# Gated cross attention and a routed feed-forward layer: two halves of a small product set apart among accumulating matmuls

## What is computed

```python
x = x + tanh(g_xattn) * xattn(layernorm(x), ctx, ctx, mask, wq, wk, wv, wo)
x = x + tanh(g_ffn)   * ffn(layernorm(x), weight, bias, gate_w, in_channel_scale, out_channel_scale)

def xattn(...):                       # 32 heads in 16 pairs
    attn = softmax(rope(q) @ rope(k).T / sqrt(128) + mask)
    return (attn @ v) in heads' order @ wo        # wo: (4096, 1024)
```

## Time and profile before

| | before |
|---|---|
| median of three executions | 1468.59 us |
| profiled execution, its own time | 1468.77 us |
| its span, first to last instruction | 1467.0 us |
| TensorE busy | 1446.3 us, 99% |
| VectorE, ScalarE, GpSimd busy | 68%, 39%, 49% |
| mean granted clock of TensorE | 0.997 |
| TensorE's share of the chain that ended last | 89% |

### The profile page before, as it was taken

One profiled execution on the slowest core, in us unless ns is written; L12 is line 12 of the kernel. 1 busy time (PEld: TensorE's weight loads), 2 busy tenths in 40 slices (PEclk: granted clock), 3 DMA queues, 4 the chain that ended last, 5 costly groups with the idle time before them and its releaser, 6 DMA issues.

```text
span 1467.0 us, 21329 instructions
## 1 busy us (share of the span) xinstructions
PE 1446.3 (99%) x6800; PEld 1197.1 (82%) x6800; DVE 998.9 (68%) x2141; ACT 570.1 (39%) x927; POOL 719.9 (49%) x594
## 2 busy tenths in 40 slices
PE   7999999999999999999999989999999999999998
PEld 6988888888888888888888867888888888877786
DVE  6858888888888888888888876636246247436653
ACT  6922222222222222222222258438348348225551
POOL 6935554554555545545555456426226226036554
PEclk9999999999999999999999999999999999999999
DMA  8822122212221222122212298888998989943321
GB/s 309 289 101 65 39 80 74 69 52 70 79 70 43 79 71 71 50 71 79 71 43 72 72 312 274 292 263 275 353 353 268 369 272 298 302 152 111 113 79 65
DMA packets 114898, 226.40 MB, mean 154 GB/s; under 512 B 12272, under 2 KB 23024, under 8 KB 114704
## 3 DMA queue, kind: packets, MB, share of 16 engines
q1 hardware_dynamic: 110224, 210.03, 44.7%
q10 hardware_dynamic: 4608, 15.53, 2.9%
HBM read 167.84 MB, written 57.67 MB: 154 GB/s over the span
## 4 chain that ended last, share of the span: by engine, by line
PE 89%; issue 3%; DVE 2%; POOL 2%; DMA 2%; SPq 1%; ACT 1%; POOLq 0%; ACTq 0%
PE bank L52 19%; PE bank L53 19%; PE bank L54 19%; PE bank L966 8%; PE bank L967 8%; PE bank L968 8%; PE bank L990 5%; POOL last_rows L1424 1%; PE bank L1005 1%; SPq L727 1%; DMA w_raw<-in_wo 1%; DVE stats L293 1%; DMA w_raw<-in_wkv 1%; DVE x_lo L324 1%; PE xt_ps L152 0%
## 5 line engine op out<-in xcount | busy, mean ns | idle before, releaser
L52 PE MATMUL bank<-x_hi,w_hi 128*128 128x512 f32 x1024 | 398.5, 389 | 0.3 <-issue 0.3
L54 PE MATMUL bank<-x_hi,w_lo 128*128 128x512 f32 x1024 | 398.3, 389 | 0.0
L53 PE MATMUL bank<-x_lo,w_hi 128*128 128x512 f32 x1024 | 398.3, 389 | 0.0
L1363 POOL TENSOR_TENSOR q_lo<-rot,q_hi 128x512 fp32r<-128x512 f32 x128 | 165.4, 1293 | 184.0 <-ACT q_hi L1126 183.1
L52 PEld LDWEIGHTS bank<-x_hi,w_hi 128*128 128x128 f32 x1024 | 192.2, 188 | 40.4 <-issue 0.5
L53 PEld LDWEIGHTS bank<-x_lo,w_hi 128*128 128x128 f32 x1024 | 192.2, 188 | 39.9
L54 PEld LDWEIGHTS bank<-x_hi,w_lo 128*128 128x128 f32 x1024 | 192.2, 188 | 39.8
L1126 ACT CAST q_hi<-rot 128x512 fp32r<-128x512 f32 x128 | 79.5, 621 | 346.2 <-DVE rot L1487 254.2
L1429 POOL TENSOR_TENSOR w_lo<-w_raw,w_hi 128x512 fp32r<-128x512 f32 x100 | 127.1, 1292 | 169.5 <-ACT w_hi L1178 169.5
L1559 DVE TENSOR_TENSOR project<-bank,project 64x512 fp32r<-64x512 f32 x128 | 87.5, 684 | 144.8 <-ACT project L1186 142.8
L1370 POOL TENSOR_TENSOR pt_lo<-pt,pt_hi 128x512 fp32r<-128x512 f32 x64 | 82.5, 1290 | 153.7 <-ACT pt_hi L1136 153.6
(11 more groups left out here) (143 smaller groups left out, 2656.4 us busy)
## 6 DMA issues: line engine op xcount, KB each, us to landing
project<-probs_scratch SPq DMA_DIRECT2D x160, 256.0 KB, 6.8
w_raw<-in_wo SPq DMA_DIRECT2D x100, 256.0 KB, 4.6
p_left<-probs_scratch SPq DMA_DIRECT2D x96, 256.0 KB, 5.7
w_raw<-in_wq SPq DMA_DIRECT2D x32, 512.0 KB, 5.2
probs_scratch<-pt_hi SPq DMA_DIRECT2D x64, 256.0 KB, 2.6
probs_scratch<-pt_lo SPq DMA_DIRECT2D x64, 256.0 KB, 3.2
last_rows<-in_x SPq DMA_DIRECT2D x8, 1024.0 KB, 8.4
x_scratch<-last_rows SPq DMA_DIRECT2D x8, 1024.0 KB, 9.1
```

The source lines that it names most:

```text
L52: pe.matmul(out, hi, rhs_hi, start=first, stop=False, **kw)
L53: pe.matmul(out, hi, rhs_lo, start=False, stop=False, **kw)
L54: return pe.matmul(out, lo, rhs_hi, start=False, stop=last, **kw)
L1363: nc.gpsimd.tensor_tensor(q_lo[:, c], rot[:, c], q_hi[:, c].bitcast(F32), ALU.subtract).then_inc(q_lo_ready, 1)
```

## The change

A helper `halves` issues, for h 0 and 1: half h of the upcoming product, if there is one, and then two of the four tiles of rows of the sum. All three kinds of phases call it. Product and sum are the same instructions as before; a sum is now two calls of `probs_times` with two tiles each, and each call issues its three waits.

In phase 0 the product also stands at another place in relation to the sum: before, product hp + 2 came behind sum hp; now its halves come in front of and in the middle of sum hp. At hp 0 the sum has already been issued, so only the product is. The other engines' and queues' orders are as before.

```diff
--- before.py
+++ after.py
@@ -971,6 +971,14 @@
                 if t == NACC - 1:
                     last.then_inc(av_done, 1)
 
+            def halves(phase, hp, upcoming, rows=True):
+
+                for h in range(2):
+                    if upcoming is not None:
+                        values_wo(upcoming, h)
+                    if rows:
+                        probs_times(phase, hp, (2 * h, 2 * h + 1))
+
             def products(i, j, steps):
 
                 for step in steps:
@@ -1066,21 +1074,16 @@
             values_wo(1, 1)
             probs_times(0, 0, (1, 2, 3))
             for hp in range(HP):
-                if hp >= 1:
-                    probs_times(0, hp)
-                if hp + 2 < HP:
-                    for h in range(2):
-                        values_wo(hp + 2, h)
+                halves(0, hp, hp + 2 if hp + 2 < HP else None, hp >= 1)
             for phase in range(1, PHASES):
                 rnd, long = phase // PB, phase % PB == 0
                 for hp in range(HP):
+                    upcoming = None
                     if long and hp + 3 < HP:
-                        for h in range(2):
-                            values_wo(rnd * HP + hp + 3, h)
+                        upcoming = rnd * HP + hp + 3
                     if not long and hp in SHORT_VW and rnd + 1 < ROUNDS:
-                        for h in range(2):
-                            values_wo((rnd + 1) * HP + SHORT_VW[hp], h)
-                    probs_times(phase, hp)
+                        upcoming = (rnd + 1) * HP + SHORT_VW[hp]
+                    halves(phase, hp, upcoming)
                     if phase == LAST:
                         first_block(hp)
```

## The result

Twenty executions of each kernel gave a median of 1472.55 us after the change (1470.20 to 1477.42) and 1469.24 us before it (1467.74 to 1473.37). The ratio is 1.002, with a 95% interval of 1.0014 to 1.0025: the change costs 2.1 to 3.7 us, 2.9 in the middle; the two medians are 3.3 us apart. The profiled execution of the changed kernel took 1471.23 us, 2.46 us more than that of before (1468.77), and its span is 1469.4 us.

The account below looks back on a forecast made before the run. TensorE was taken as the bound. Gaps of 1.68 + 0.81 + 1.15 = 3.64 us replacing 1.62 gave +2.0, taken as +2.2: 1471.0 from the profile, 1470.8 from the median, stated 1470.9; range 1468.7 to 1473.3 us.

Parts of the forecast that it names:

- the forecast's own case: Whole kernel: the main case, 1470.8 to 1471.1 us, chance 0.50.
- the replay: Phase 0 from 872.58 us, recomputed with the rows' durations: 3.64 us of gaps in place of 1.62, +2.0 us.
- (3,0): Phase 0, product 3, half 0: waits for the drain of (2,0) until 874.18, gap 1.60 + 0.08 us.
- (4,0): Phase 0, product 4, half 0: waits for the drain of (3,0) until 879.07, gap 0.73 + 0.08 us.
- (11,0): Phase 0, product 11, half 0: waits for the drain of (10,0) until 908.78, gap 1.07 + 0.08 us.
- a later landing, a delay passed through the loads: Phase 0: drain (4,1), about 0.3 us later, can pass through the weights' loads to pair 11; upper value +2.3.
- (11,1) no longer waits: Phase 0, product 11, half 1: comes 2.04 us later, so its gap of 0.76 us goes.
- phases 1 to 7 cost nothing: Phases 1 to 7: parted halves cost and give nothing, as products there have slack.
- Extra waits at 0: All sums: 381 more waits on TensorE, taken as 0, upper bound 1.3 us.
- The clock rival: Phase 0, after 873 us: the granted clock falls to 0.5; 1472 to 1473.7, about 1472.4 us, chance 0.25.
- the half one: Phase 0, within the clock rival's 0.25: a fall half as long as 6.8 us, +1.0 us besides the 2.2.
- the DMA's matter: Phase 0, weights of pair 11: issued at 898.00, in ScalarE's hands at 905.32, not expected to get earlier.

Follow-up runs that it names:

- The second lot: The changed kernel run again, unmodified, six executions against the kernel before: 1474.31 us, ratio 1.0031.
- whole, no gaps: Kernel before with rows' load later, pair 2's weights earlier, ScalarE draining product 15 before casting weights of pairs 16 and 17: 1466.92 us, ratio 0.9988.
- parted, no gaps: "changed in place, early weights" with ScalarE draining product 15 before casting weights of pairs 16 and 17: 1467.08 us, ratio 0.9983.
- changed, gap filled: Changed kernel with seven useless matmuls between products (2,1) and (3,0) of phase 0: 1471.74 us, ratio 1.0016.
- changed, gap lengthened: Changed kernel with TensorE also waiting, ahead of (3,0), until both halves of product 2 are drained: 1475.13 us, ratio 1.0034.
- rows later: 1 MB load of rows of x moved to step 10 of phase 0: in the kernel before 1473.66 us, in the changed one 1473.04 us.
- changed in place, early weights: Changed kernel with products in their old step, product 15 whole, rows' load later, pair 2's weights loaded earlier: 1473.27 us, ratio 1.002.
- the last two kernels: "parted, no gaps" and "whole, no gaps": 1467.08 and 1466.92 us.

## Why the prediction was right, point by point

*The number.* The forecast was 1470.9 us, +2.3 on the median known then; the measured median is 1472.55 us, inside the range but above the 1470.8 to 1471.1 that the forecast's own case allowed. Of the 1.65 us, 0.65 are the median of before, which is 1469.24 us over twenty executions and not 1468.59. The other 1.0 is what the medians differ by (3.3) beyond my 2.3. The profiles are nearer: by the tail the change costs 2.4 us in one and 1.8 in the other, where I had +2.0 from the replay and took 2.2. The rest of the medians, 0.9 to 1.5 us, is in no gap of the profiles.

*Phase 0 is the only price.* Right, and to the place. (3,0) was forecast for 874.18 and started at 874.20; (4,0) for 879.07, and started at 879.09; the drain of (3,0) was taken up at 876.92 although its product ran 1.1 us earlier than before (874.20 against 875.31), as the replay said (876.91). That the places and not the parting cost the time is shown by the traces of the kernels with one part each: the move alone has the gap at (3,0), the parting alone has none at (3,0) or (4,0). The ratios agree, 1.0016 for the move and 1.0007 with 1 inside its interval for the parting, but their intervals overlap and would not decide it alone.

*(11,0).* The step was right and the term was too small: 1.49 us instead of 1.15. The drain of (10,0) ended at 908.33 + 0.69 = 909.02 rather than 908.63, because ScalarE got the weights of pair 11 at 905.70 rather than 905.32. My reason for a later landing, a delay passed through the loads, is not what happened: SyncE issued them at 897.58, 0.42 us earlier than before (898.00 in the earlier trace rows), and they took 8.1 us to ScalarE's hands instead of 7.3. I had also written that nothing ahead of them gets earlier. What made the transfer longer stays open, and the landing is no constant of the kernel. The same kernel in its second profile had 0.84 + 0.07 us there, and the one with only the later phases changed had 1.08 + 0.08 with the old order. So it is luck that the forecast of +2.2 us agrees with this profile to 0.2 us: the one term has a spread of about 0.6 us from one execution to the next.

*(11,1) no longer waits, phases 1 to 7 cost nothing.* Right in the trace. The kernel with only these phases changed leaves a doubt: its median is 1.7 us above before, and of the 1.3 us by which the tail of its profile is longer, 1.1 lie in phase 0.

*Extra waits at 0.* Right as far as can be told: three times as many gave a ratio of 1.0003, with 1 inside the interval.

*The clock rival.* Neither profiled execution of the changed kernel shows it: behind the gap at (3,0) their clock is at 1.00. The other executions may, as far as a mean clock tells. Of the first 20, 14 had a mean clock of 0.997 or more and a median of 1471.8 us, +2.6; the other 6 had 1474.6. If these 6 owe their time to the clock, forecast and rival were both true, each of a part of the executions, and that would account for most of what the medians are apart beyond the profiles. The second lot, with two slow executions at a mean clock of 0.997 and 0.998, does not fit this simply. The count over all runs, by the longest gap in phase 0 of the profiled execution:

| kernel | longest gap, us | executions with mean clock of 0.996 or less |
|---|---|---|
| before, in all three batches | 0.8 | 7 of 91 |
| sums in four calls; whole, no gaps; parted, no gaps | 0.8 or less | 1 of 34 |
| parted in place; later phases only | 1.1 | 4 of 24 |
| changed, gap filled (longest then at pair 11) | 1.4 | 1 of 12 |
| changed, both lots | 1.6 | 8 of 26 |
| moved whole | 1.6 | 4 of 11 |
| changed, gap lengthened | 2.9 | 5 of 6 |
| rows later: changed; changed in place, early weights; before | 1.7, 3.9, 4.1 | 7 of 11, 7 of 11, 10 of 10 |

The mean is a coarse sign. It also carries the stretch at half rate ahead of phase 0, which 13 of the 14 profiles have, 6.8 us long in each; the profiled execution with the lengthened gap lacked it and reads 0.999 in spite of its fall. In the kernel with later rows, early weights and ScalarE's old order the time doesn't follow it: the seven executions that bear the sign have a median of 1473.45 us and the other four 1473.2. The clock did fall behind gaps in the moved and in the lengthened kernel, as their stretches show. The five falls seen inside the projection lasted 3.4 us each, half of the 6.8 that I had read ahead of phase 0, so one costs at most 1.7 us: of the rival's two cases, the half one. That the 6 executions owe their time to a fall is only argued from the counts.

The Trainium skill ("TensorE: Matmul & The Clock Gate", Part 1) says that the gate runs free of the kernel's start, so the place of a clock change varies from run to run. The traces agree: behind the gap of 2.1 us ahead of phase 0, with the same work ahead of it, the fall came 0.1 us after the gap's end in the profile of before and 2.8 us after it in the changed kernel's. The falls behind (3,0) say less. The gap of 1.6 us was followed by a fall in the moved kernel's profile and by none in the two of the changed one, but in these the stretch at half rate reached to 869.9 and 870.3 us and left no gap of note at pair 2, so the gap at (3,0) stood alone.

*What I left out.* Sum 15 was in none of my cases, yet it waited in four of the experiments, for 0.6 to 4.1 us. I had looked only for what a product waits for, and not for the last sum, which has no product ahead of it. And in costing the late weights as "the DMA's matter" I took the DMA order as given; that order, together with ScalarE's, is what the last two kernels improved.

## What to carry to other kernels

When two operations of an in-order queue change places, first ask whether the one that moves up is ready where it now stands: here the replay of two drains gave both starts to 0.02 us, while parting the halves did nothing that the medians show. A queue that stands for a late load should not hold a drain that is urgent behind it; loads move their lateness with them, so look at which loads are next in line before moving one. Where an edit opens gaps on TensorE like the 1.6 us here, the clock can fall behind them in some executions and not in others, so compare several executions and not one profile.

## What the hardware showed unexpectedly

- TensorE's granted clock fell to half after gaps of 0.8, 0.6 and 1.6 us in a row (moved kernel, 876 to 878 us: 0.50), though the gap ahead of phase 0 that had seemed its example was 2.1 us long.
- The stretch at half rate ahead of phase 0 moves from one execution to the next and keeps its length. It lay at 860.3 to 867.1 us in the profile of before, as the clocks of 0.57 and 0.72 in the earlier trace rows say (the prediction had 860.0 to 866.9), and at 863.0 to 869.9 in that of the changed kernel, with the same work ahead of it. The later place cost no time, because pair 2's weights were awaited anyway: (2,1) started at 871.84 against 871.81. Rows of the changed kernel:

```profile
862.00:864.00 2.00, 0.98 (x3) 0.48 (x3) 1.59 (x3) 1.72 (x3) 1.21 (x2) 0.76 1.08 389
...
866.00:868.00 2.00, 2.00 (x6) 1.52 (x6) 0.69 (x1) 0.00 (x0) 0.00 (x0) 0.50 1.02 340
868.00:870.00 2.00, 2.00 (x7) 1.57 (x6) 0.00 (x0) 1.60 (x3) 0.99 (x1) 0.53 1.04 379
870.00:872.00 2.00, 2.00 (x10) 1.51 (x9) 1.38 (x2) 1.94 (x4) 2.00 (x3) 1.00 0.45 147
```

- A semaphore wait on TensorE that is already met cost nothing that 1143 of them could show.
